# Moving work between VectorE, GpSimd and ScalarE in a state-space mixer, with taps over two blocks, a ring of six products and a new order

## The chip, the cores and the metric

The kernel runs on one core of one Trainium2 chip. The metric is the device time of one execution in microseconds; the kernel before is given by three runs and one profiled execution. The engines are named TensorE (PE in the rows; PEld is its weight load), VectorE (DVE), ScalarE (ACT), GpSimd (POOL) and SyncE (SP, which only issues DMAs here).

## The reference

The input is a batch of 8 sequences of 256 tokens with 256 features. After a layer norm two branches read it, and their results are added to the input: a state-space mixer and an MLP of six blocks.

```python
zxbcdt = hidden_states @ W_in                  # z, x: 4096 channels each; B, C: 128; dt: 64 heads
xbc = _causal_conv1d(xbc, conv_w, conv_b)      # 4 taps over time, then silu
dt = jax.nn.softplus(dt + dt_bias)
dA_cs = jnp.cumsum(dt * A, axis=2)
L = jnp.exp(jnp.where(mask, dA_cs[i] - dA_cs[j], -jnp.inf))       # causal decay
Y = jnp.einsum('bcign,bcjgn,bcijgh,bcjghp->bcighp', Cm, Bm, L, dtx) # plus the states of earlier chunks
y = (Y + D * x) * _silu(z)
yn = y * jax.lax.rsqrt(jnp.mean(y * y) + EPS) * norm_w
x = x + yn @ W_out + _L0_ffn_ref(xn)           # 6 x (W1, gelu, W2, residual, layer norm)
```

The kernel does not run the chunked scan: a sequence is only 256 tokens long, so it takes the whole causal 256 x 256 decay matrix of each sequence and head at once.

## The kernel before

The program has three parts: `prepare` (layer norm, B, C, dt and their running sums), `mix` (the mixer) and `mlp`. The change touches `mix` alone.

**Tiles, blocks, products.** `mix` goes over 32 tiles `c` of 128 inner channels, which are two heads (HPT = 2) of 64. Within a tile the 2048 tokens are four blocks `b` of 512 (NB = 4), each two sequences `s` of 256 (SPB = 2). What this document calls a product is one pair (b, s): for both heads, the causal decays times C.B of one sequence, eight per tile. The causal matrix of 256 x 256 is held as 128 partitions (source tokens) by LW = 384 columns: first source half against all 256 targets, then second source half against the last 128. Two heads make 768 columns. The columns 128 to 256 of each head lie wholly below the diagonal.

**The way of a tile.** TensorE projects x (`project_x`) and z (`project_z`), each block six matmuls 512 wide into one of two PSUM banks `pa`; ScalarE turns the x bank into the convolution's first term (`conv0`, L847), VectorE adds the three other taps (`tap`, helper `conv_tap`, L517) straight from the bank, ScalarE applies silu (`silu_x`, L856), and for z silu out of the bank (`silu_z`, L865). A bank is free again after the third tap, or after the silu of z. TensorE transposes x to token rows (`tokens`, L750), ScalarE copies them (`copy_tokens`, L892).

Beside it run the decays: VectorE writes the exponents of a product (`exponents`, L989: for each head one instruction 256 and one 128 wide) into the ring `dec`, clipped by the constant `floor`, which lies in PSUM; ScalarE takes the exponential in place (`decays`, L874, 768 wide); GpSimd multiplies by the masked C.B in `gmat` (`times_g`, L681, 768 wide). TensorE then multiplies with the token rows (`outputs`, L769), VectorE adds D x (`add_dx`, L1004) and gates with silu(z) (`gate`, L1017), ScalarE squares (`square`, L883) and rounds (`high`, L919), GpSimd sums the squares (`add_square`, L690) and forms the low part (`low`, L670). Every second tile TensorE begins the rows of W_out for the pair of tiles before (`output_rows`, L787 to L789, twelve matmuls 256 wide in a piece), and VectorE adds them to `acc` (`add_rows`, L1030). Weights are split in a high and a low part by `w_hi`, `o_hi` (ScalarE) and `w_lo`, `o_lo` (GpSimd, L654 and L662); `scale_o` (L901) applies the norm's weight.

**What sets the order.** Each engine has a function `step(c)` in which the order of one tile's steps is written out by hand, with tiles mixed: a step of tile c stands beside steps of c - 1 and c + 1. The engines run their lists independently and wait for semaphore counts. `wait_past` leaves a wait out where the count is zero or less. `dec` holds four products (two blocks), so `exponents` waits for the product of two blocks back. SyncE loads the rows of running sums `srow` in two halves of a tile, 512 KB for each head, once VectorE has written the exponents of that half (`arg_done`); its queue is in order with the other loads of `body`. The weights of the MLP's first layer go to `w1raw`, loaded at the mixer's start.

## Time and profile before

| | us |
|---|---|
| median of 3 runs | 1522.66 (1520.12 to 1525.63) |
| profiled execution, its own time | 1524.01 |
| its span | 1522.2 |
| busy over the span: TensorE / VectorE / ScalarE / GpSimd | 1448.4 / 1255.7 / 1087.8 / 1119.7 |
| mixer's first exponents / its last instruction on VectorE | 75.0 / 947.0 |

The profiled span is shown as 40 slices of 38 us, each digit the busy tenths of a slice:

```profile
DVE  6899999999999999999999993567666776776752
ACT  5679888888988888898888883656555555655542
POOL 4279999999999999999999997645263451634650
PEclk9899999999999999999999997999999999999999
```

The first two slices are `prepare`, the next twenty-two the mixer, the rest the MLP. TensorE's busy time says little here, since the ends of its matmuls are modelled: its demand is read from the starts. An operation on VectorE, ScalarE and GpSimd is shown with its own length, and the next one may start some 0.05 to 0.1 us before it ends, so a row's cost in a full queue is the distance between two starts.

### The profile page before, as it was taken

To read this page: it belongs to the slowest core of one execution; us is meant where nothing else is said; L and a number is where in the kernel's file an instruction comes from. 1 tells how busy PE (TensorE), PEld (TensorE's weight loads), DVE (VectorE), ACT (ScalarE), POOL (GpSimd) and SP (SyncE) were. 2 spreads that over 40 slices of the span, in tenths; PEclk is the share of its full clock that TensorE was granted. 3 is DMA by queue.
4 is the path that set the end of the run, shared out by engine and by line. 5 is a ranking of instruction groups with operands and counts; after the bars stand their busy time and mean duration, and the time that the engine had idled before them with its cause. 6 is when DMAs were issued, how large, how long until landed. Compare 5 with 4: busy or idle time off the path is not lost. (4 is left out here: it accounts for less than half of the span.)

```text
span 1522.2 us, 27373 instructions
## 1 busy us (share of the span) xinstructions
PE 1448.4 (95%) x9432; PEld 1188.4 (78%) x9432; DVE 1255.7 (82%) x2534; ACT 1087.8 (71%) x1764; POOL 1119.7 (74%) x763
## 2 busy tenths in 40 slices
PE   6789999999999999999999997999999999999998
PEld 5556777777777777777777776899998989989988
DVE  6899999999999999999999993567666776776752
ACT  5679888888988888898888883656555555655542
POOL 4279999999999999999999997645263451634650
PEclk9899999999999999999999997999999999999999
DMA  4233323232332323232232210300101001020011
GB/s 142 72 130 105 97 79 105 83 105 91 105 98 74 102 90 105 91 105 98 70 100 96 98 56 26 128 1 29 39 2 66 0 28 38 0 79 0 1 56 42
DMA packets 50159, 107.62 MB, mean 71 GB/s; under 512 B 13248, under 2 KB 25792, under 8 KB 48448
## 3 DMA queue, kind: packets, MB, share of 16 engines
q1 hardware_dynamic: 50048, 106.21, 21.3%
q8 instruction: 61, 1.00, 0.3%
q14 instruction: 50, 0.41, 0.1%
HBM read 101.47 MB, written 4.72 MB: 70 GB/s over the span
## 5 line engine op out<-in xcount | busy, mean ns | idle before, releaser
L681 POOL TENSOR_TENSOR mix_dec<-mix_dec,gmat 128x768 f32<-128x768 f32 x256 | 471.1, 1862 | 17.1 <-ACT mix_dec L874 17.1
L1411 DVE TENSOR_TENSOR mlp_hlo<-mlp_h,mlp_hhi 128x512 fp32r<-128x512 f32 x192 | 209.6, 1093 | 181.9 <-ACT mlp_hhi L1343 181.5
L989 DVE SCALAR_TENSOR_TENSOR mix_dec<-srow,tokpar,mix_floor 128x256 f32<-128x256 f32 (+1 forms) x1024 | 348.9, 408 | 11.9 <-PE mix_py L769 11.9
L1338 ACT ACTIVATE mlp_h<-mlp_p,mlp_b1c 128x512 f32<-128x512 f32 x192 | 132.1, 688 | 203.4 <-PE mlp_p L501 197.5
L517 DVE SCALAR_TENSOR_TENSOR xt<-mix_pa,conv,xt 128x510 f32<-128x510 f32 x372 | 262.3, 740 | 12.3 <-ACT xt L847 9.6
L501 PE MATMUL mix_pa<-xhi,whi 128*128 128x512 f32 x496 | 212.8, 429 | 20.5 <-DVE xt L517 19.6
L769 PE MATMUL mix_py<-mix_dec,mix_xtok 128*64 128x256 f32 (+1 forms) x2048 | 215.0, 339 | 15.9 <-ACT mix_xtok L892 8.6
L1304 PE MATMUL mlp_p<-mlp_w2hi,mlp_hhi 128*128 128x256 f32 x768 | 218.6, 285 | 3.2 <-DVE acc L1470 3.2
L1306 PE MATMUL mlp_p<-mlp_w2hi,mlp_hlo 128*128 128x256 f32 x768 | 216.5, 282 | 0.0
L769 PEld LDWEIGHTS mix_py<-mix_dec,mix_xtok 128*64 128x64 f32 x2048 | 128.4, 137 | 112.2 <-issue 57.8
L1305 PE MATMUL mlp_p<-mlp_w2lo,mlp_hhi 128*128 128x256 f32 x768 | 216.0, 281 | 0.0
L874 ACT ACTIVATE mix_dec<-mix_dec 128x768 f32<-128x768 f32 x256 | 212.9, 844 | 3.8 <-DVE mix_dec L989 2.8
L501 PE MATMUL mix_pa<-xlo,whi 128*128 128x512 f32 x496 | 196.7, 397 | 0.0
L501 PE MATMUL mix_pa<-xhi,wlo 128*128 128x512 f32 x496 | 196.6, 396 | 0.0
L690 POOL TENSOR_TENSOR mix_sqacc<-mix_sqacc,mix_sq 128x512 f32<-128x512 f32 x128 | 166.6, 1302 | 4.5 <-ACT mix_sq L883 4.5
L670 POOL TENSOR_TENSOR mix_glo<-mix_yg,mix_ghi 128x512 fp32r<-128x512 f32 x128 | 167.4, 1308 | 1.9 <-ACT mix_ghi L919 1.9
L501 PE MATMUL mlp_p<-xhi,mlp_w1hi 128*128 128x512 f32 x384 | 153.5, 400 | 2.0 <-POOL mlp_w1lo L1199 2.0
L1304 PEld LDWEIGHTS mlp_p<-mlp_w2hi,mlp_hhi 128*128 128x128 f32 x768 | 144.6, 188 | 13.4 <-DVE mlp_hlo L1411 3.6
L501 PE MATMUL mlp_p<-xlo,mlp_w1hi 128*128 128x512 f32 x384 | 153.3, 399 | 0.0
L501 PE MATMUL mlp_p<-xhi,mlp_w1lo 128*128 128x512 f32 x384 | 153.2, 399 | 0.0
L787 PE MATMUL mix_po<-mix_ohi,mix_ghi 128*128 128x256 f32 x512 | 148.6, 290 | 3.5 <-POOL mix_glo L670 2.1
L1305 PEld LDWEIGHTS mlp_p<-mlp_w2lo,mlp_hhi 128*128 128x128 f32 x768 | 144.6, 188 | 6.1
(130 smaller groups left out, 3207.8 us busy)
## 6 DMA issues: line engine op xcount, KB each, us to landing
srow<-cs_rows SPq DMA_DIRECT2D x128, 512.0 KB, 4.6
wraw<-w_xz SPq DMA_DIRECT2D x32, 256.0 KB, 5.6
w1raw<-w SPq DMA_DIRECT2D x6, 1028.0 KB, 4.8
mlp_w2raw<-w SPq DMA_DIRECT2D x6, 1024.0 KB, 6.7
mix_oraw<-w_out SPq DMA_DIRECT2D x16, 257.0 KB, 5.5
prep_hid<-hidden SPq DMA_DIRECT2D x4, 512.0 KB, 6.6
xn_rows<-prep_hid SPq DMA_DIRECT2D x4, 512.0 KB, 2.9
mlp_res<-xn_rows SPq DMA_DIRECT2D x1, 2048.0 KB, 10.2
```

What stands on the lines that cost most here:

```text
L501: last = pe.matmul(dst, w[:, k, :], x[:, k, cols], start=(i == 0), stop=(i == len(passes) - 1))
L517: return dve.scalar_tensor_tensor(d[:, :, k:SEQ], s[:, :, 0:SEQ - k], weight, d[:, :, k:SEQ], ALU.mult, ALU.add)
L670: pool.tensor_tensor(glo[:, t.par, cols(b)], yg[:, b, :], ghi[:, t.par, cols(b)].bitcast(F32), ALU.subtract).then_inc(glo_done, 1)
L681: pool.tensor_tensor(d, d, g, ALU.mult).then_inc(g_done, 1)
L690: pool.tensor_tensor(sqacc[:, cols(b)], sqacc[:, cols(b)], sq[:, b % 2, :], ALU.add).then_inc(sq_added, 1)
L769: last = pe.matmul(py[b % 2][hp, i], xtok[:, b % 2, 2 * s + j, hp], dec[:, b % 2, s, h, m], start=(j == 0), stop=(j == 1))
L874: act.activation(d, d, ACT.Exp, scale=-1.0).then_inc(dec_done, 1)
L989: last = dve.scalar_tensor_tensor(dec[:, b % 2, s, h, k], srow[:, half, h, i], tokpar[:, tile, HPT * c + h:HPT * c + h + 1], floor[:, 0:1] ...
L1304: pe.matmul(dst, hhi[:, j, k], w2hi[:, j, :], start=(j == 0), stop=False)
L1305: pe.matmul(dst, hhi[:, j, k], w2lo[:, j, :], start=False, stop=False)
L1306: last = pe.matmul(dst, hlo[:, j, k], w2hi[:, j, :], start=False, stop=(j == KH - 1))
L1411: dve.tensor_tensor(hlo[:, j, :], h[:, j % 4, :], hhi[:, j, :].bitcast(F32), ALU.subtract).then_inc(hlo_done, 1)
```

## The change

All of it is in `mix`, on four engines and the DMA queue.

```diff
+        DVE_G = [3]
+        POOL_G = [u for u in range(SPB * NB) if u not in DVE_G]
...
+        spare = w1raw[:, 0:SPB * HPT * LW].rearrange("p (s h i) -> p s h i", s=SPB, h=HPT)
...
+        def ring(c, b):
+            n = (NB * c + b) % 3
+            return dec[:, n] if n < 2 else spare
...
             load(0, d_par, dcol[:, 0], d_in[0])
-            sp.dma_start(w1raw[:], w1[0]).then_inc(w1_in, 16)
...
-                            sp.wait_ge(arg_done, SPB * (NB * c + NB // 2 * (half + 1)))
+                            sp.wait_ge(dec_done, SPB * (NB * c + NB // 2 * (half + 1)))
...
+            last = max(n for n in range(NB * NCT) if n % 3 == 2)
+            sp.wait_ge(y_done, SPB * (last + 1))
+            sp.dma_start(w1raw[:], w1[0]).then_inc(w1_in, 16)
...
-                pe.wait_ge(g_done, SPB * n + s + 1)
+                if u in DVE_G:
+                    pe.wait_ge(dve_g_done, len(DVE_G) * t.c + DVE_G.index(u) + 1)
+                else:
+                    pe.wait_ge(pool_g_done, len(POOL_G) * t.c + POOL_G.index(u) + 1)
...
             def decays(c, b, s):
...
-                d = dec[:, b % 2, s].rearrange("p h i -> p (h i)")
-                act.activation(d, d, ACT.Exp, scale=-1.0).then_inc(dec_done, 1)
+                if s == 0:
+                    d = ring(c, b)[:, s].rearrange("p h i -> p (h i)")
+                    act.activation(d, d, ACT.Exp, scale=-1.0).then_inc(dec_done, 1)
+                    return
+                half, i1 = b // 2, b % 2 * BLK + s * SEQ + P
+                tile = b * TPB + 2 * s
...
+                for h in range(HPT):
...
+                    act.activation(ring(c, b)[:, s, h, P:SEQ], srow[:, half, h, i1:i1 + P], ACT.Exp,
+                                   bias=tokpar[:, tile, HPT * c + h:HPT * c + h + 1], scale=-1.0)
+                d = ring(c, b)[:, s].rearrange("p h (k i) -> p h k i", i=P)[:, :, 0:3:2, :]
+                act.activation(d, d, ACT.Exp, scale=-1.0).then_inc(dec_done, 1)
...
-            def tap(c, b, k):
+            def taps(c, i, k):
...
-                conv_tap(dve, xt[:, t.par, cols(b)], pa[b % 2][:],
-                         conv[:, t.par, TAPS - 1 - k:TAPS - k], k).then_inc(done, 1)
+                conv_tap(dve, xt[:, t.par, 2 * i * BLK:2 * (i + 1) * BLK], pab[:],
+                         conv[:, t.par, TAPS - 1 - k:TAPS - k], k).then_inc(done, 2)
...
-                wait_past(dve, y_done, m - 2 * SPB + 1)
+                wait_past(dve, y_done, m - 3 * SPB + 1)
...
+                    first = SEQ if s == 0 else P
...
+            def times_g(c, b, s):
...
+                dve.wait_ge(dec_done, SPB * (NB * t.c + b) + s + 1)
+                d = ring(c, b)[:, s]
+                g = gmat[:, b * SPB + s, :].unsqueeze(1).broadcast_to([P, HPT, LW])
+                dve.tensor_tensor(d, d, g, ALU.mult).then_inc(dve_g_done, 1)
```

In words: product (1, 1) of each tile, number 3 of eight, is multiplied by the masked C.B on VectorE and no longer on GpSimd, both operands in SBUF; TensorE waits for one of two counts, one for each of these engines. In the second product of each block (s = 1) VectorE no longer writes the exponents of the columns 128 to 256; ScalarE computes their exponential from the row of running sums with the token's number as bias. The two banks become one tensor `pab`, and each tap is one instruction over both. The ring holds three blocks, the third in the memory of `w1raw`, whose load comes at the end of the mixer. The load of the next rows waits for the exponentials of the half instead of its exponents. And each engine's `step(c)` is written in a new order. Three places of it follow; `w1raw` in the rows of after is the third block of the ring.

VectorE, the middle of a tile, before: the taps of blocks 2 and 3, one bank a row, between D x, gate and one product's exponents.

```order
L517 SCALAR_TENSOR_TENSOR xt<-mix_pa0,conv,xt 128x2x255 [waits conv0_done]
L1004 SCALAR_TENSOR_TENSOR mix_py0<-xt,mix_dcol,mix_py0 128x512 [waits mix_y_done,mix_d_in0]
L517 SCALAR_TENSOR_TENSOR xt<-mix_pa0,conv,xt 128x2x254 [waits tap1_done]
L1017 TENSOR_TENSOR mix_yg<-mix_py0,zt 128x512 [waits mix_sq_done,mix_glo_done,z_done,mix_yd_done]
L989 SCALAR_TENSOR_TENSOR mix_dec<-srow,tokpar,mix_floor 128x256 [waits mix_y_done]
L989 SCALAR_TENSOR_TENSOR mix_dec<-srow,tokpar,mix_floor 128x128
L989 SCALAR_TENSOR_TENSOR mix_dec<-srow,tokpar,mix_floor 128x256
L989 SCALAR_TENSOR_TENSOR mix_dec<-srow,tokpar,mix_floor 128x128
L517 SCALAR_TENSOR_TENSOR xt<-mix_pa1,conv,xt 128x2x255 [waits conv0_done]
L517 SCALAR_TENSOR_TENSOR xt<-mix_pa0,conv,xt 128x2x253 [waits tap2_done]
L517 SCALAR_TENSOR_TENSOR xt<-mix_pa1,conv,xt 128x2x254 [waits tap1_done]
L517 SCALAR_TENSOR_TENSOR xt<-mix_pa1,conv,xt 128x2x253 [waits tap2_done]
```

The same engine after, from the end of block 3's first exponents on: the product by C.B (L1025) stands between the two products of exponents, and the taps take both banks at once.

```order
L1012 SCALAR_TENSOR_TENSOR w1raw<-srow,tokpar,mix_floor 128x128
L1025 TENSOR_TENSOR mix_dec<-mix_dec,gmat 128x768 [waits mix_dec_done]
L1012 SCALAR_TENSOR_TENSOR w1raw<-srow,tokpar,mix_floor 128x128 [waits mix_y_done]
L1012 SCALAR_TENSOR_TENSOR w1raw<-srow,tokpar,mix_floor 128x128 x3
L1036 SCALAR_TENSOR_TENSOR mix_py0<-xt,mix_dcol,mix_py0 128x512 [waits mix_y_done,mix_d_in0]
L517 SCALAR_TENSOR_TENSOR xt<-mix_pab,conv,xt 128x4x255 [waits conv0_done]
L1049 TENSOR_TENSOR mix_yg<-mix_py0,zt 128x512 [waits mix_sq_done,mix_glo_done,z_done,mix_yd_done]
L517 SCALAR_TENSOR_TENSOR xt<-mix_pab,conv,xt 128x4x254 [waits tap1_done]
L1036 SCALAR_TENSOR_TENSOR mix_py1<-xt,mix_dcol,mix_py1 128x512 [waits mix_y_done]
L517 SCALAR_TENSOR_TENSOR xt<-mix_pab,conv,xt 128x4x253 [waits tap2_done]
```

What moved: the exponents of block 3 stand ahead of the tile's second taps, and the operation L1025, which waits for ScalarE, is new among them. The six rows of taps are three.

ScalarE, the end of block 3, before:

```order
L919 CAST mix_ghi<-mix_yg 128x512 [waits mix_o_done,mix_gated]
L892 COPY mix_xtok<-mix_pt 128x512 [waits mix_y_done,mix_xtok_done]
L874 ACTIVATE mix_dec<-mix_dec 128x768 [waits mix_arg_done]
L847 ACTIVATE xt<-mix_pa1,conv 128x512 [waits mix_yd_done,px_done]
L919 CAST mix_ghi<-mix_yg 128x512 [waits mix_o_done,mix_gated]
L874 ACTIVATE mix_dec<-mix_dec 128x768 [waits mix_arg_done]
```

and after:

```order
L904 ACTIVATE mix_sq<-mix_yg 128x512 [waits mix_sq_added,mix_gated]
L940 CAST mix_ghi<-mix_yg 128x512 [waits mix_o_done,mix_gated]
L856 ACTIVATE xt<-mix_pab,conv 128x512 [waits mix_yd_done,px_done] x2
L884 ACTIVATE mix_dec<-mix_dec 128x768 [waits mix_arg_done]
L892 ACTIVATE mix_dec<-srow,tokpar 128x128 [waits mix_arg_done]
L892 ACTIVATE mix_dec<-srow,tokpar 128x128
L895 ACTIVATE mix_dec<-mix_dec 128x2x2x128
```

What moved: the biases of blocks 2 and 3 (`conv0`) stand together ahead of the exponentials of block 3, and the second exponential is three instructions.

GpSimd, around the first six products of a tile, before:

```order
L681 TENSOR_TENSOR mix_dec<-mix_dec,gmat 128x768 [waits mix_dec_done]
L670 TENSOR_TENSOR mix_glo<-mix_yg,mix_ghi 128x512 [waits mix_ghi_done]
L681 TENSOR_TENSOR mix_dec<-mix_dec,gmat 128x768 [waits mix_dec_done] x2
L690 TENSOR_TENSOR mix_sqacc<-mix_sqacc,mix_sq 128x512 [waits mix_sq_added,mix_sq_done]
L681 TENSOR_TENSOR mix_dec<-mix_dec,gmat 128x768 [waits mix_dec_done] x3
L654 TENSOR_TENSOR wlo<-wraw,whi 128x512 [waits mix_w_hi_done]
L690 TENSOR_TENSOR mix_sqacc<-mix_sqacc,mix_sq 128x512 [waits mix_sq_added,mix_sq_done]
```

and after:

```order
L687 TENSOR_TENSOR mix_dec<-mix_dec,gmat 128x768 [waits mix_dec_done] x2
L687 TENSOR_TENSOR w1raw<-w1raw,gmat 128x768 [waits mix_dec_done]
L687 TENSOR_TENSOR mix_dec<-mix_dec,gmat 128x768 [waits mix_dec_done]
L676 TENSOR_TENSOR mix_glo<-mix_yg,mix_ghi 128x512 [waits mix_ghi_done]
L687 TENSOR_TENSOR mix_dec<-mix_dec,gmat 128x768 [waits mix_dec_done] x2
L696 TENSOR_TENSOR mix_sqacc<-mix_sqacc,mix_sq 128x512 [waits mix_sq_added,mix_sq_done]
L660 TENSOR_TENSOR wlo<-wraw,whi 128x512 [waits mix_w_hi_done]
L676 TENSOR_TENSOR mix_glo<-mix_yg,mix_ghi 128x512 [waits mix_ghi_done]
```

What moved: the sum of squares that stood between the products is gone from there, a product is missing (the one on VectorE), and the low part of the block before stands ahead of product (2, 1), waiting for ScalarE's rounded part.

## Rows read from the trace of the kernel before

**Rows 1.** Stretch, length; busy us of PE, PEld, DVE, ACT, POOL; clock, DMA, GB/s.

```profile
400.00:600.00 200.00, 195.28 (x1336) 150.11 (x1334) 195.59 (x421) 173.35 (x275) 196.87 (x132) 1.00 0.28 90
```

**Rows 2.** Timeline of ScalarE: start us, length us, engine, line, operation, count.

```profile
424.80 0.78 ACT L847 ACTIVATE xt<-mix_pa,conv 128x512 f32<-128x512 f32 x1 [0.30 <-PE mix_pa L501]
...
451.50 0.78 ACT L847 ACTIVATE xt<-mix_pa,conv 128x512 f32<-128x512 f32 x1 [0.30 <-PE mix_pa L501]
```

**Rows 3.** One line: ns min/median/max, first and last start; then VectorE's timeline.

```profile
L681 POOL TENSOR_TENSOR mix_dec<-mix_dec,gmat x256: 1808/1862/1925, 77.4 to 924.0; 128x768 f32<-128x768 f32 x128
...
947.04 0.17 DVE L1069 TENSOR_SCALAR meansq<-mix_pt 128x16 f32<-128x16 f32 x1 [2.78 <-PE mix_pt L822]
```

**Rows 4.** Waits, 400 to 608 us: who for whom, us in total, times, longest.

```profile
POOL mix_dec L681 <- ACT mix_dec L874: 3.1, 4, 0.8
...
DVE xt L517 <- ACT xt L847: 1.7, 7, 0.2
...
PE mix_pa L501 <- DVE xt L517: 5.2, 8, 0.7
```

**Rows 5.** Timeline of TensorE.

```profile
406.52 0.66 PE L750 MATMUL mix_pt<-ident,xt 128*128 128x128 f32 x4
...
406.94 0.36 PE L787 MATMUL mix_po<-mix_ohi,mix_ghi 128*128 128x256 f32 x1
...
408.45 0.39 PE L501 MATMUL mix_pa<-xhi,whi 128*128 128x512 f32 x1
...
409.94 1.63 PE L769 MATMUL mix_py<-mix_dec,mix_xtok 128*64 128x256 f32 x16
...
411.50 0.66 PE L750 MATMUL mix_pt<-ident,xt 128*128 128x128 f32 x4
...
415.12 0.43 PE L501 MATMUL mix_pa<-xhi,whi 128*128 128x512 f32 x1
...
416.56 0.39 PE L501 MATMUL mix_pa<-xhi,whi 128*128 128x512 f32 x1
```

**Rows 6.** Timeline of GpSimd.

```profile
434.91 1.88 POOL L681 TENSOR_TENSOR mix_dec<-mix_dec,gmat 128x768 f32<-128x768 f32 x1
436.72 1.30 POOL L662 TENSOR_TENSOR mix_olo<-mix_oraw,mix_ohi 128x512 fp32r<-128x512 f32 x1
```

**Rows 7.** Timeline of VectorE and of GpSimd in the MLP.

```profile
984.79 0.69 DVE L1411 TENSOR_TENSOR mlp_hlo<-mlp_h,mlp_hhi 128x512 fp32r<-128x512 f32 x1 [2.14 <-ACT mlp_hhi L1343]
...
1063.36 2.40 POOL L1218 TENSOR_TENSOR mlp_res<-mlp_u,mlp_grow 128x1024 f32<-128x1024 f32 x1 [1.50 <-DVE mlp_u L1441]
...
1065.84 2.72 POOL L1220 TENSOR_TENSOR mlp_res<-mlp_res,mlp_grow 128x1024 f32<-128x1024 f32 x1
...
1063.83 2.48 DVE L1411 TENSOR_TENSOR mlp_hlo<-mlp_h,mlp_hhi 128x512 fp32r<-128x512 f32 x1 [0.55 <-ACT mlp_hhi L1343]
```

**Rows 8.** Groups of instructions, 400 to 608 us (busy, mean ns), and VectorE's timeline.

```profile
L989 DVE SCALAR_TENSOR_TENSOR mix_dec<-srow,tokpar,mix_floor 128x256 f32<-128x256 f32 x126 | 59.8, 475 | 2.1 <-PE mix_py L769 2.1
...
L989 DVE SCALAR_TENSOR_TENSOR mix_dec<-srow,tokpar,mix_floor 128x128 f32<-128x128 f32 x126 | 43.0, 341 | 0.0
...
400.17 2.69 DVE L517 SCALAR_TENSOR_TENSOR xt<-mix_pa,conv,xt 128x508 f32<-128x508 f32 x4
...
402.78 0.68 DVE L1017 TENSOR_TENSOR mix_yg<-mix_py,zt 128x512 f32<-128x512 f32 x1
```

**Rows 9.** Timeline of ScalarE.

```profile
406.85 0.84 ACT L874 ACTIVATE mix_dec<-mix_dec 128x768 f32<-128x768 f32 x1
...
407.58 0.63 ACT L883 ACTIVATE mix_sq<-mix_yg 128x512 f32<-128x512 f32 x1
...
408.61 0.92 ACT L901 ACTIVATE mix_oraw<-mix_oraw 128x256 f32<-128x256 f32 x2
...
409.42 0.61 ACT L919 CAST mix_ghi<-mix_yg 128x512 fp32r<-128x512 f32 x1
```

**Rows 10.** Loads (part 6 of the page): count, KB each, us to landing.

```profile
w1raw<-w SPq DMA_DIRECT2D x6, 1028.0 KB, 4.8
```

More of the change, by code:

```diff
@@ L533, in mix @@
         wraw, whi, wlo, w_in, conv, conv_in, srow, srow_in, xt, zt, stages, w1raw, w1_in, meansq):
-    DVE_G = [(0, 0)]
-    POOL_G = [(b, s) for b in range(NB) for s in range(SPB) if (b, s) not in DVE_G]
     with ExitStack() as ctx:
@@ L562, in mix @@
         onesq = sb("onesq", [P, 2])
-        pa = [ps(f"pa{i}") for i in range(2)]
+        pab = ctx.enter_context(nc.psum_tensor("mix_pab", [P, 2 * BLK], F32))
+        pa = [pab[:, i * BLK:(i + 1) * BLK] for i in range(2)]
         pt = ps("pt")
@@ L769, in outputs @@
                         last = pe.matmul(py[b % 2][hp, i], xtok[:, b % 2, 2 * s + j, hp],
-                                         dec[:, b % 2, s, h, m], start=(j == 0), stop=(j == 1))
+                                         ring(c, b)[:, s, h, m], start=(j == 0), stop=(j == 1))
                 last.then_inc(y_done, 1)
@@ L792, in step @@
             def step(c):
+                project_x(c, 1)
+                output_rows(c - 1, 0)
+                tokens(c - 1, 1)
+                output_rows(c - 1, 1)
+                tokens(c - 1, 2)
+                outputs(c - 1, 0, 0)
+                outputs(c - 1, 0, 1)
+                project_x(c, 2)
+                project_x(c, 3)
+                output_rows(c - 1, 2)
+                outputs(c - 1, 1, 0)
+                outputs(c - 1, 1, 1)
+                tokens(c - 1, 3)
+                output_rows(c - 1, 3)
                 outputs(c - 1, 2, 0)
-                tokens(c - 1, 3)
                 outputs(c - 1, 2, 1)
+                tokens(c, 0)
                 project_z(c, 0)
@@ L931, in step @@
                 conv0(c + 1, 0)
-                high(c - 1, 1)
                 conv0(c + 1, 1)
@@ L983, in exponents @@
                     dve.wait_ge(srow_in[half], 16 * HPT * (t.c + 1))
-                wait_past(dve, y_done, m - 2 * SPB + 1)
+                wait_past(dve, y_done, m - 3 * SPB + 1)
                 for h in range(HPT):
-                    for j, i, k in ((0, slice(i0, i0 + SEQ), slice(0, SEQ)),
+                    first = SEQ if s == 0 else P
+                    for j, i, k in ((0, slice(i0, i0 + first), slice(0, first)),
                                     (1, slice(i0 + P, i0 + SEQ), slice(SEQ, LW))):
@@ L989, in exponents @@
                         last = dve.scalar_tensor_tensor(
-                            dec[:, b % 2, s, h, k], srow[:, half, h, i],
+                            ring(c, b)[:, s, h, k], srow[:, half, h, i],
                             tokpar[:, tile, HPT * c + h:HPT * c + h + 1],
@@ L993, in exponents @@
                 last.then_inc(arg_done, 1)
+            def times_g(c, b, s):
+                if not 0 <= c < NCT:
+                    return
+                t = tile_of(c)
+                dve.wait_ge(dec_done, SPB * (NB * t.c + b) + s + 1)
+                d = ring(c, b)[:, s]
+                g = gmat[:, b * SPB + s, :].unsqueeze(1).broadcast_to([P, HPT, LW])
+                dve.tensor_tensor(d, d, g, ALU.mult).then_inc(dve_g_done, 1)
             def add_dx(c, b):
```

148 lines of the change are left out of this document (66 added, 82 removed).

## Prediction

> **What bounds the kernel now.** I read the page's table of slices first: VectorE, ScalarE and GpSimd are dense up to the 24th slice and thin behind it, so the program is a mixer of some 870 us and an MLP of some 575 us, and the change touches the mixer alone. The view by stretches shows it in the steady middle [rows 1]: of 200 us GpSimd is busy 196.87, VectorE 195.59, ScalarE 173.35, and TensorE 195.28 by a modelled end. Then I took one tile's length: the same ScalarE row comes again after 451.50 - 424.80 = 26.70 us [rows 2]. The products run from 77.4 to 924.0 us and the mixer to 947 [rows 3]; 846.6 us is 31 tiles of 26.70 and the 19 us of the last. So each 0.1 us of a tile is worth 3.1 us of the kernel.
>
> Per tile the busy shares become GpSimd 0.984 x 26.70 = 26.28 us, VectorE 26.11, ScalarE 23.14. The waits in 208 us [rows 4] are few: GpSimd 3.1 us for the exponentials, 0.4 per tile; that and its 26.28 us make up the 26.70. GpSimd is therefore the bound, VectorE is 0.2 us behind it, and TensorE waits 5.2 us (0.65 per tile) for the taps to free a bank. TensorE's own demand is read off from where its groups start [rows 5]: the first projection of a run takes 1.49 us (408.45 to 409.94), one that follows another 1.44 (415.12 to 416.56); twelve output-row matmuls 1.51 (406.94 to 408.45); four transposes 0.42 (406.52 to 406.94); two C.B products 1.56 (409.94 to 411.50). The granted clock is 1.00 in that stretch [rows 1], the upper level, so these are its prices.
>
> **The change, part by part**, each as microseconds per tile.
>
> *One product of eight to VectorE.* GpSimd loses one of its eight. Its price there is the distance of two starts, 436.72 - 434.91 = 1.81 [rows 6]. GpSimd: 26.28 - 1.81 = 24.47. No row of before has VectorE do this product. The nearest is VectorE's subtraction with both inputs in SBUF in the MLP, 512 wide: 0.69 us [rows 7]. The exponents give the slope: 475 - 341 = 134 ns for 128 elements [rows 8], so 768 wide is 0.69 + 0.27 = 0.96, and 0.88 to the next start, since neighbours overlap by 0.08 (four taps are busy for 2.69 us, and the next operation starts after 2.61 [rows 8]). But [rows 7] show a second thing. The same subtraction, started at 1063.83 while GpSimd's 2.40 us operation of 1063.36 ran, took 2.48 and ended 0.55 us behind GpSimd's end; GpSimd's next, started at 1065.84, took 2.72. They exclude each other for the whole instruction. In the mixer of before this never shows, since each VectorE operation there has one input in PSUM. So the product costs VectorE 0.88 and a wait between 0 and one GpSimd product, 1.8. Walking the new order in starts from the third tap of blocks 0 and 1 at 0: the product is due at 3.1; GpSimd is by then 0.3 us from the end of its fourth product, and waits behind it for the high part of the gated block. I take 0.3, keep 0 and 1.8, and charge GpSimd nothing, as VectorE's 0.88 falls into a gap of about 1.1 us in which GpSimd waits for ScalarE; without that gap it costs GpSimd 0.9, for which its 1.2 us below TensorE's demand has room.
>
> The Trainium skill, "SBUF — State Buffer", section "Who interferes with whom", speaks against handing work between these two: VectorE with two SBUF inputs and a GpSimd instruction that reads SBUF hold the pair of ports for a whole instruction, and the second fully blocks. By that rule alone the move gives GpSimd 1.81 - 0.88 and not 1.81. The rows of the MLP agree with the rule.
>
> *Half of the exponentials below the diagonal to ScalarE.* VectorE's second product of each block computes 128 instead of 256 exponents for both heads: 4 blocks x 2 x 0.134 = 1.07 saved. ScalarE splits that block's exponential: two 128-wide ones with bias and scale from the row, and a 512-wide one for the rest in place of 768. Spacings of starts [rows 9]: 768 wide 0.73 (406.85 to 407.58); 512 wide 0.51 (two rows from 407.58 to 408.61, halved); with a pointer operand and 256 wide 0.405 (0.81 for two from 408.61 to 409.42). By ScalarE's slope of 0.22/256 per element, 128 wide is 0.405 - 0.11 = 0.29. So 2 x 0.29 + 0.51 - 0.73 = 0.36 more, four times: 1.44. Its bounds are 1.1 (short ones at 0.25) and 2.4 (at 0.41, the 256-wide price). ScalarE: 23.14 + 1.44 = 24.6.
>
> The Trainium skill, "ScalarE: Activation LUTs", section "What ACT_TABLE_LOAD costs", gives a 128-wide ACTIVATE with pointer bias 280 + 0.833 x 128 = 387 ns, of which neighbours hide 93. That is 0.294 each and would leave the sum as it is; no run yet shows the 128-wide form.
>
> *Taps over two blocks.* Twelve taps of 0.65 (2.61 / 4) become six. A doubled one adds 510 elements at 1.047 ns: 0.65 + 0.53 = 1.19. VectorE: 7.83 - 7.12 = 0.71 saved. What it costs is in the banks: both are given back only with the third tap.
>
> *Sum for VectorE:* 26.11 - 1.07 - 0.71 + 0.88 + 0.3 = 25.5, with 25.2 and 27.0 as ends.
>
> *Ring of six.* The exponents wait for a product six back, not four. The wait it lifts is the 2.1 us for TensorE's products at the end of the first row of [rows 8], 0.27 per tile, already in the gaps between busy and 26.70. The third block of the ring lies in the buffer of the MLP's first weights, whose 1 MB load moves from the mixer's start to the product two blocks before its end. Behind that are two blocks of products, their gates and the last rows, over 10 us, while this load lands in 4.8 us [rows 10], so I cost it at nothing; were it bare it would be 5 us, once. The row loads now wait for the exponential on ScalarE instead of the exponents on VectorE, a few us later: by the walk the first half is issued at 26 us and wanted at 37, and it is no larger than the load of [rows 10].
>
> *New order.* On TensorE the work is the same, in other groups: 3 runs of projections (3 x 1.49 + 5 x 1.44 = 11.67), output rows 4 x 1.51 = 6.04, products 4 x 1.56 = 6.24, transposes 4 x 0.42 = 1.68: 25.63 us. Of four engines this is now the largest, so it is the floor: TensorE 25.63, VectorE 25.5, ScalarE 24.6, GpSimd 24.5. Walked through with these prices, the loop that returns to itself is: third tap done, projections x 2 and 3, taps of blocks 2 and 3, four z projections, two products, projections x 0 and 1, bias on ScalarE, three taps. The work put between fills TensorE's waits to within 0.1 to 0.3 us at three places (x 2, z 0, and the tap behind x 1). Before, the kernel ran 0.4 above its largest sum. I take 0.15 above, 25.8, and keep 25.63 and 26.1.
>
> *Ends.* At the start six instead of four products of exponents precede the first taps, 1.8 us later (by [rows 8] a full one is 2 x (0.395 + 0.261) = 1.31 and a lessened one 1.04, so 7.05 for 5.24); at the end GpSimd has three operations of 1.25 between its last product and TensorE's last rows, four before. Net 0.5 us more.
>
> **Sum.** 31 x (26.70 - 25.8) = 27.9, less 0.5: 27.4 us. The profiled execution took 1524.0 us, its span 1522.2; it would become 1496.6. It stands 1.3 above the median of the three runs shown, so against the median the forecast is 1495 us, 1.8% faster.
>
> **Rivals.** (a) *The shared banks bind.* ScalarE gets no rest between the bias of block 1 and that of block 3: by the walk the latter is ready 0.5 us before the tap wants it. If the short exponentials cost 0.41, three of these blocks lie there and add 3 x 0.24 = 0.7; the doubled tap cannot start on the first bank alone, as a single one could. The tile becomes 26.2 to 26.6, say 26.4: 1514 us. For it: VectorE waits for this bias in the trace of before too, 1.7 us in 208 [rows 4]. Against: by the sum ScalarE still rests 1.2 us in a tile of 25.8, and the tap's 0.5 us have to be used up first.
>
> (b) *VectorE becomes the bound through the exclusion, and the kernel is slower.* The place is the product between two blocks of exponents; behind it on the same queue stand the exponents of block 3 and the tap for which TensorE waits. If the phase is such that it always meets a fresh GpSimd product, VectorE needs 27.0, and with the old 0.2 of gaps 27.2: 31 x 0.5 = 15.5 us slower, 1538. It decides from a wait of 1.3 us on. Against it: such a wait makes VectorE late, while GpSimd is 1.2 us under the floor and drifts ahead into its gap, where the port is free.
>
> (c) *It does not do what it says*: GpSimd's relief is real but VectorE stays as full as it was, at 26.5 with its waits: within 0.3%, 1520.
>
> (d) *Better*: the new order leaves TensorE no wait and a tile takes 25.5: 1486.
>
> **Chances.** Forecast (25.6 to 26.1 us per tile, 1486 to 1503) 0.60; (a) 0.16; (b) 0.09; (c) 0.07; (d) 0.08. A measurement of this kernel tells about 0.3% from no change. Faster is the forecast, (a) and (d): 0.84; same is (c), 0.07; slower (b), 0.09. The range reaches from (d) to the far side of (a), 1484 to 1517, and leaves out (b) and (c), 0.16.
>
> **What will show it.** Right: a tile of 25.8 between two equal rows in the middle; GpSimd's busy share at 0.95 or below with its waits on ScalarE, TensorE with almost none; the doubled tap at 1.27 us a piece; the short exponential near 0.38; VectorE's product between 0.96 and 1.3 on average. A product above 2 us with VectorE at 99% means (b); TensorE waiting over 0.5 us per tile for taps behind a late bias means (a). The MLP should keep its length to a microsecond. I would be wrong altogether if the row loads came too late at the exponents of a new tile, or if GpSimd's products grew beside the VectorE one.

## The result, and the profile after

The kernel after takes 1488.86 us, median of four runs (1488.68 to 1494.12); the kernel before, four runs beside it, 1521.66 (1520.12 to 1525.63). The ratio is 0.979, its 95% interval 0.9775 to 0.9799: 2.1% faster, where 1.8% was forecast (1495 us, range 1484 to 1517). The profiled execution of after took 1488.68 us, with a span of 1486.9.

First the view by stretches, over the same 200 us as [rows 1], and the waits of 400 to 608 us (who for whom: us in total, times, longest), to be held beside [rows 4]:

```profile
400.00:600.00 200.00, 198.11 (x1364) 159.20 (x1363) 197.08 (x400) 189.67 (x348) 192.21 (x130) 1.00 0.30 100
...
ACT zt L874 <- PE mix_pab L501: 7.8, 8, 1.1
POOL mix_glo L676 <- ACT mix_ghi L940: 7.3, 8, 1.1
...
PEld mix_pab L501 <- DVE xt L517: 2.4, 8, 0.3
DVE xt L517 <- ACT xt L856: 2.1, 8, 0.3
PE mix_pt L755 <- ACT mix_xtok L913: 1.7, 5, 0.4
```

GpSimd fell from 196.87 to 192.21 busy, and now waits for ScalarE's rounded part, about 0.9 us per tile. ScalarE rose from 173.35 to 189.67; it still waits for TensorE's z projections (7.8 us, before 10.3), while its wait for TensorE's token transposes, 14.7 us before, is gone from the list. What is left on TensorE's side are 1.7 us for token copies and short waits of its weight loads. Second, one tile's length. Each exponential table load of ScalarE stands once in a tile; the timeline of ScalarE (start, length) gives three tiles:

```profile
409.43 1.28 ACT L884 ACT_TABLE_LOAD   x1
...
434.90 1.28 ACT L884 ACT_TABLE_LOAD   x1
...
460.75 1.28 ACT L884 ACT_TABLE_LOAD   x1
...
486.22 1.28 ACT L884 ACT_TABLE_LOAD   x1
```

The distances are 25.47, 25.85 and 25.47: the tile alternates, where before it was 26.70 each time [rows 2]. Two tiles are 51.32, the mean about 25.67. Third, the mixer's ends on VectorE, its first exponents and its last instruction (before: 75.0 and 947.04, [rows 3]):

```profile
73.19 3.98 DVE L1012 SCALAR_TENSOR_TENSOR mix_dec<-srow,tokpar,mix_floor 128x256 f32<-128x256 f32 x13
...
914.06 0.17 DVE L1096 TENSOR_SCALAR meansq<-mix_pt 128x16 f32<-128x16 f32 x1 [2.77 <-PE mix_pt L831]
```

So of the 35.3 us between the two profiled spans (1522.2 and 1486.9) the mixer gave 872.0 - 840.9 = 31.1, the part ahead of it 1.8 and the MLP 2.4 (575.2 and 572.8), though no instruction of those two was changed.

Fourth, the new operations: VectorE with the doubled taps and the product (L1025), then GpSimd at the same time, then ScalarE's split exponential.

```profile
441.94 1.26 DVE L517 SCALAR_TENSOR_TENSOR xt<-mix_pab,conv,xt 128x1012 f32<-128x1012 f32 x1
...
443.71 1.38 DVE L1012 SCALAR_TENSOR_TENSOR w1raw<-srow,tokpar,mix_floor 128x256 f32<-128x256 f32 x4
445.01 1.55 DVE L1025 TENSOR_TENSOR mix_dec<-mix_dec,gmat 128x768 f32<-128x768 f32 x1
446.48 1.11 DVE L1012 SCALAR_TENSOR_TENSOR w1raw<-srow,tokpar,mix_floor 128x128 f32<-128x128 f32 x4
...
442.08 3.66 POOL L687 TENSOR_TENSOR mix_dec<-mix_dec,gmat 128x768 f32<-128x768 f32 x2
446.83 1.29 POOL L676 TENSOR_TENSOR mix_glo<-mix_yg,mix_ghi 128x512 fp32r<-128x512 f32 x1 [1.09 <-ACT mix_ghi L940]
...
413.10 0.68 ACT L892 ACTIVATE mix_dec<-srow,tokpar 128x128 f32<-128x128 f32 x2
413.68 0.62 ACT L895 ACTIVATE mix_dec<-mix_dec 128x512 f32<-128x512 f32 x1
```

The product begins 0.73 us before GpSimd's pair ends at 445.74, is itself 1.55 long and ends 0.82 behind that end, in the gap of 1.09 that the prediction had named.

### The profile page after: what moved, and what is told of

Same layout as the page of the kernel before. It is cut to its first block and busy times, and to the rows that moved or that the text cites. A ratio compares the mean times of both kernels' runs of the same rounds, so it can differ in the third digit from the quotient of the medians.

```text
span 1486.9 us, 27692 instructions
## 1 busy us (share of the span) xinstructions
PE 1424.6 (96%) x9432; PEld 1198.3 (81%) x9432; DVE 1237.1 (83%) x2380; ACT 1126.7 (76%) x2020; POOL 1064.4 (72%) x731
## 5 line engine op out<-in xcount | busy, mean ns | idle before, releaser
L1438 DVE TENSOR_TENSOR mlp_hlo<-mlp_h,mlp_hhi 128x512 fp32r<-128x512 f32 x192 | 218.1, 1138 | 175.8 <-ACT mlp_hhi L1370 175.6
L687 POOL TENSOR_TENSOR mix_dec<-mix_dec,gmat 128x768 f32<-128x768 f32 x151 | 278.1, 1856 | 10.4 <-ACT mix_dec L884 6.8
L517 DVE SCALAR_TENSOR_TENSOR xt<-mix_pab,conv,xt 128x1020 f32<-128x1020 f32 x186 | 236.2, 1270 | 12.7 <-ACT xt L856 9.2
L1012 DVE SCALAR_TENSOR_TENSOR mix_dec<-srow,tokpar,mix_floor 128x128 f32<-128x128 f32 (+1 forms) x688 | 214.2, 373 | 1.9 <-PE mix_py L778 1.9
L501 PE MATMUL mix_pab<-xhi,whi 128*128 128x512 f32 x496 | 206.0, 415 | 2.0 <-DVE xt L517 0.2
L501 PE MATMUL mix_pab<-xlo,whi 128*128 128x512 f32 x496 | 196.5, 396 | 0.0
L501 PE MATMUL mix_pab<-xhi,wlo 128*128 128x512 f32 x496 | 196.5, 396 | 0.0
L676 POOL TENSOR_TENSOR mix_glo<-mix_yg,mix_ghi 128x512 fp32r<-128x512 f32 x128 | 164.7, 1299 | 31.4 <-ACT mix_ghi L940 30.4
L797 PE MATMUL mix_po<-mix_olo,mix_ghi 128*128 128x256 f32 x512 | 146.0, 285 | 0.0
L798 PE MATMUL mix_po<-mix_ohi,mix_glo 128*128 128x256 f32 x512 | 145.7, 285 | 0.0
L1333 PEld LDWEIGHTS mlp_p<-mlp_w2hi,mlp_hlo 128*128 128x128 f32 x768 | 144.5, 188 | 0.0
```

What stands on the lines that cost most here:

```text
L501: last = pe.matmul(dst, w[:, k, :], x[:, k, cols], start=(i == 0), stop=(i == len(passes) - 1))
L517: return dve.scalar_tensor_tensor(d[:, :, k:SEQ], s[:, :, 0:SEQ - k], weight, d[:, :, k:SEQ], ALU.mult, ALU.add)
L676: pool.tensor_tensor(glo[:, t.par, cols(b)], yg[:, b, :], ghi[:, t.par, cols(b)].bitcast(F32), ALU.subtract).then_inc(glo_done, 1)
L687: pool.tensor_tensor(d, d, g, ALU.mult).then_inc(pool_g_done, 1)
L797: pe.matmul(dst, ghi[:, e, r], olo[:, e, :], start=False, stop=False)
L1012: last = dve.scalar_tensor_tensor(ring(c, b)[:, s, h, k], srow[:, half, h, i], tokpar[:, tile, HPT * c + h:HPT * c + h + 1], floor[:, 0:1] ...
```

## The experiments

All times are medians of the runs made, with the ratio to the kernel before and its interval; the kernel before gave 1521.65 to 1522.21 beside them. "Tile" is the distance of exponential table loads in the middle of the mixer.

**Theory:** each of the three vector engines has a total per tile, the longest set 26.70 before, and the moves bring all of them under TensorE's. **Rivals:** the order and the ring alone do it; the exclusion of VectorE and GpSimd through SBUF eats the gain.

### Single moves undone in the kernel after

*pool8*: the product back on GpSimd.

```diff
-        DVE_G = [3]
+        DVE_G = []
...
                 times_g(c, 1, 0)
+                times_g(c, 1, 1)
                 times_g(c, 2, 0)
...
                 exponents(c - 1, 3, 0)
-                times_g(c - 1, 1, 1)
                 exponents(c - 1, 3, 1)
```

> The changed kernel with one part undone: product (1,1) goes back to GpSimd, behind (1,0); VectorE has none. Theory (sums): GpSimd is again the largest at 24.5 + 1.8 = 26.3 us per tile and waits once for ScalarE's rounded part (0.9 us per tile after the change), so a tile takes 26.3 to 27.2 and the kernel 1489 + 31 x (0.6 to 1.5) = 1508 to 1536 us, GpSimd at 97% or more. Rival (the order and the ring brought the gain, not this part): 1489 to 1494, with TensorE still without waits.

Measured: 1513.41 us, 0.9945 (0.9928 to 0.9962). Tiles alternate between 25.8 and 26.9, mean 26.34. The stretch 400 to 600, then the same for *fullexp*, which gives the 128 columns below the diagonal back to VectorE (1507.79 us, 0.9906, 0.9889 to 0.9922; tile 26.26):

```profile
400.00:600.00 200.00, 196.23 (x1346) 155.18 (x1346) 184.44 (x386) 184.22 (x337) 199.76 (x134) 1.00 0.31 98
```

```profile
400.00:600.00 200.00, 193.89 (x1343) 156.10 (x1343) 199.27 (x391) 175.42 (x279) 193.41 (x127) 1.00 0.30 98
```

```diff
-                if s == 0:
+                if True:
...
-                    first = SEQ if s == 0 else P
+                    first = SEQ
```

> The changed kernel with one part undone: VectorE writes all exponents, ScalarE takes each exponential in one 768-wide piece. Theory (sums): VectorE was at 25.3 us busy of 25.67 per tile and gets 1.07 back, so it becomes the bound at 26.4 and the kernel takes 1489 + 31 x 0.75 = 1512 us (1505 to 1520), while ScalarE falls below 90%. Rival: ScalarE is what limits the changed kernel (it is busy 95% there), and relieving it of 1.4 us pays for VectorE's 1.07: 1485 to 1495.

In the first GpSimd has 199.76 of 200 us, in the second VectorE 199.27: undoing one move fills exactly the engine that gets the work back. Both moves are needed, and each is worth about 0.6 us of a tile, since the other engine is just behind.

*onetaps*: twelve single taps again, for six doubled ones.

```diff
             def taps(c, i, k):
+                tap(c, 2 * i, k)
+                tap(c, 2 * i + 1, k)
...
-                dve.wait_ge(before, NB * c + 2 * i + 2)
-                conv_tap(dve, xt[:, t.par, 2 * i * BLK:2 * (i + 1) * BLK], pab[:],
-                         conv[:, t.par, TAPS - 1 - k:TAPS - k], k).then_inc(done, 2)
+                dve.wait_ge(before, NB * c + b + 1)
+                conv_tap(dve, xt[:, t.par, cols(b)], pa[b % 2],
+                         conv[:, t.par, TAPS - 1 - k:TAPS - k], k).then_inc(done, 1)
```

> The changed kernel with one part undone: each tap is two instructions again, one per bank, in the same place. Theory (sums): VectorE gets 0.7 us per tile back, 26.0 instead of 25.3 busy, so the kernel takes 1489 + 31 x (0.4 to 0.7) = 1501 to 1511 us. Rival (joining the banks costs time, because a bank is given back late): single taps free the first bank 0.6 us sooner and start on the first bias alone, which pays for their length: 1480 to 1492.

Measured: 1490.35 us (1488.89 to 1496.95), 0.9783 (0.9766 to 0.9799), the same time as after; tile 25.67. VectorE's row and its groups of 400 to 608 us (busy, mean ns):

```profile
400.00:600.00 200.00, 198.78 (x1369) 159.27 (x1368) 200.00 (x446) 190.29 (x347) 193.75 (x130) 1.00 0.30 98
...
L1029 DVE TENSOR_TENSOR mix_dec<-mix_dec,gmat 128x768 f32<-128x768 f32 x5 | 6.1, 1217 | 0.0
...
L517 DVE SCALAR_TENSOR_TENSOR xt<-mix_pab,conv,xt 128x510 f32<-128x510 f32 (+2 forms) x100 | 69.6, 753 | 0.0
```

The taps cost 69.6 us instead of 62.2, and VectorE is full to the last tenth, but not longer than TensorE's tile. The price is smaller than the row suggests, since neighbours overlap. From start to next start, over sixteen tiles between 330 and 760 us, the taps cost 7.85 us a tile against 7.31 in after: 0.54 more, not 0.71. VectorE paid for it with the 0.26 us per tile that it waited in after, with 0.09 of a gap behind the gates, and with a product that waits less for GpSimd (1.09 against 1.25 from start to start). My expectation of 1501 to 1511 missed. The time is what its rival gave; whether the rival's reason, a start on the first bias alone, has a part in the lost wait, these rows do not tell. *dve_probe*, with joined taps, lost the same wait: one more 128-wide exponent operation on VectorE per tile, its result unused.

```diff
                 last.then_inc(arg_done, 1)
+                if (b, s) == (3, 1):
+                    last = dve.scalar_tensor_tensor(
+                        floor[:, P:2 * P], srow[:, half, 0, i],
+                        tokpar[:, tile, HPT * c + h:HPT * c + h + 1],
+                        floor[:, 0:1].broadcast_to([P, k.stop - k.start]), ALU.subtract, ALU.max)
```

> The changed kernel with one more 128-wide exponent instruction on VectorE in block 3 of each tile, written to unused PSUM, 0.26 us more work per tile. Theory (TensorE is the floor, VectorE 0.3 us below it): 1489 to 1492. Rival (VectorE is the floor, its waits being only the exclusion's): 1489 + 31 x 0.26 = 1497.

Measured: 1493.41 us (1489.36 to 1499.84), 0.98 (0.9785 to 0.9815), tiles 25.47 and 25.86 as in after. The median lies between the theory's 1489 to 1492 and the rival's 1497, and the four runs spread over 10 us, so the time decides nothing. The tile does: the extra operation costs 0.26 us from start to start, VectorE's wait of 0.26 per tile is gone, and the tile is as long as in after.

### The floor, and the longer of two tiles

*pe_probe*: block 3 is transposed twice, by my estimate 0.36 us more for TensorE.

```diff
-                for k in range(b * TPB, (b + 1) * TPB):
+                for k in [j for _ in range(1 + (b == 3)) for j in range(b * TPB, (b + 1) * TPB)]:
```

> The changed kernel with TensorE's four transposes of block 3 done twice, 0.36 us more work per tile and nothing else. Theory (TensorE's demand is the floor): a tile takes 0.3 to 0.36 longer, 1489 + 31 x 0.33 = 1498 to 1500 us. Rival (VectorE's or ScalarE's row of work is what a tile takes): TensorE has the room, 1489 to 1491.

Measured: 1498.51 us, 0.9843; the tile is 25.90 each time. Against 25.47 and 25.87 that is 0.43 in the shorter tile and 0.03 in the longer. In pe_probe the two sets of transposes take 0.84 us (452.71 to 453.55) where one takes 0.41 in after, so 0.43 is the probe's whole price: the shorter tile is TensorE's own. The longer has 0.4 us of something else. TensorE's timeline of after shows what. First the shorter tile, then the longer:

```profile
425.68 1.52 PE L778 MATMUL mix_py<-mix_dec,mix_xtok 128*64 128x256 f32 x16
427.13 0.66 PE L755 MATMUL mix_pt<-ident,xt 128*128 128x128 f32 x4
...
451.15 1.52 PE L778 MATMUL mix_py<-mix_dec,mix_xtok 128*64 128x256 f32 x16
453.01 0.63 PE L755 MATMUL mix_pt<-ident,xt 128*128 128x128 f32 x4 [0.35 <-ACT mix_xtok L913]
```

Transposes come 1.45 us behind the products, or 1.86 when TensorE waits for ScalarE's copy of the tokens before. Only every second tile scales W_out (L922, two operations, 0.90 us busy), and they stood ahead of this copy. *scale_late* puts them behind it:

```diff
                 decays(c, 2, 1)
-                scale_o(c + 1)
                 square(c - 1, 2)
                 copy_tokens(c, 2)
...
                 high(c - 1, 3)
+                scale_o(c + 1)
                 silu_z(c + 1, 0)
```

> The changed kernel with one step moved on ScalarE: the scaling of the output weights (two 256-wide rows, every second tile) from behind the exponentials of block 2 to just ahead of the silu of z block 0, where ScalarE waits about 1 us for TensorE. The changed kernel's tiles take 25.47 and 25.87 us in turn. Theory (in the longer tile ScalarE's unbroken row of work is late by the scaling, so TensorE waits 0.35 us for the copied tokens): all tiles take 25.47, so 16 x 0.4 = 6 us less than the changed kernel, 1482 to 1484 us. Rival (the longer tile comes from GpSimd's low part of the weights or from TensorE's own demand of 25.6): no change, 1488 to 1490.

Measured: 1486.03 us (1484.86 to 1492.10, five runs), 0.9768 (0.9749 to 0.9786), some 3 us below after, though the intervals overlap. I had expected 1482 to 1484 with every tile at 25.47. The tile is 25.48 and 25.60, so 0.27 of the 0.40 went, and the wait for the copy is gone from the list of 400 to 608 us. The 0.13 that stays lies in TensorE's row behind the same products: there the four transposes take 0.51 us to the next start and not 0.41, and the projections behind them 5.81 and not 5.78; no run says why.

```profile
435.02 1.28 ACT L884 ACT_TABLE_LOAD   x1
...
460.62 1.28 ACT L884 ACT_TABLE_LOAD   x1
...
486.09 1.28 ACT L884 ACT_TABLE_LOAD   x1
```

### The ring

*ring4*: the new order with the old ring of two blocks.

```diff
-            n = (NB * c + b) % 3
-            return dec[:, n] if n < 2 else spare
+            return dec[:, b % 2]
...
-                wait_past(dve, y_done, m - 3 * SPB + 1)
+                wait_past(dve, y_done, m - 2 * SPB + 1)
```

> The changed kernel with one part undone: the ring holds four products, the exponents wait for the product of two blocks back. Theory: the new order needs the third block. By the starts of the changed kernel the exponents of block 1 are due some 2.5 us before the product of block 3 of the tile before, for which they would wait, and this stands ahead of the next taps: 2 to 4 us per tile, 1550 to 1610 us. Rival (the ring only lifted the 0.27 us per tile of waits that were there before): 1489 to 1500.

Measured: 1965.04 us, 1.291 (1.289 to 1.293); the tile is 40.95. The waits of 400 to 608 us:

```profile
DVE mix_dec L1011 <- PE mix_py L777: 78.4, 20, 7.3
POOL mix_dec L686 <- ACT mix_dec L883: 50.6, 13, 8.8
PEld mix_pab L501 <- DVE xt L517: 43.0, 10, 7.8
```

VectorE's exponents wait for TensorE's product four back, 78.4 us in 208 or 15.4 per tile, and the tile grew by 15.3; behind them on the queue stand the taps for which TensorE's projections wait. The new order lets the exponents run further ahead than a ring of four can hold. I had priced the wait and not the loop that it closes, so the expected 1550 to 1610 was far off. The prediction had costed the ring at nothing but 0.27 us of waits; in truth the new order cannot do without it. What a ring of six gives in the old order no run shows.

### Order without moves, moves without order

*order_only* is after with the product on GpSimd, full exponents and single taps (the three edits above together). *b_dveprod* and *b_both* start from the kernel before. The first moves the product from GpSimd's step to VectorE's; the second does that and adds the lessened exponents (last line), with the split exponential of the change in `decays` and the row loads behind the exponentials. Both keep the single taps:

```diff
                 times_g(c, 1, 0)
-                times_g(c, 1, 1)
...
                 exponents(c, 2, 1)
+                times_g(c, 1, 1)
                 add_rows(c, 1)
...
+                first = SEQ if s == 0 else P
```

> The kernel after with all four moved loads undone at once: product (1,1) on GpSimd, full exponents on VectorE, single taps. The ring of six and the new order alone remain. Theory (each engine of vectors has its own total, and the longest sets the tile): GpSimd is again at the total it had with its product back, 26.3 us a tile, VectorE has 26.26 less the product's 1.1 plus 0.3 for the taps, about 25.5. So the tile is 26.3 to 26.45 and the time 1508 to 1519, as with the product alone back; VectorE waits, and ScalarE's busy time in 400 to 600 falls to about 170. Rival (order and ring bring nothing without the moves): tile 26.70, 1520 to 1524.

> The kernel before with one edit: product (1,1) on VectorE, behind the exponents of (2,1); old order, ring of four, full exponents, single taps. Theory (VectorE has no room: it was busy 195.6 of 200 us before): VectorE's total of 26.1 takes another 1.1, so the tile is 26.9 to 27.4 and the time 1530 to 1545, slower than before; GpSimd has waits. Rival (GpSimd alone bound the kernel before): tile 26.0 to 26.4, time 1500 to 1513. Third possibility, from what the ring of four did in the new order: the wait for a product two blocks back closes a loop, and the tile grows past 28, over 1560.

> The kernel before with product (1,1) on VectorE and the exponential of the 128 columns below the diagonal on ScalarE for s = 1, in the old order with the ring of four and single taps: the moves without ring and order. Theory (the moves make the room, the order turns it into time): VectorE has 26.1 plus 1.1 less 8 x 0.134 = 26.1 us of work, so at best 26.2 to 26.7 a tile, with waits for C.B products of two blocks back: 1508 to 1525. Rival 1 (the moves alone do it): tile 25.7, 1488 to 1495. Rival 2 (the ring of four closes a loop as in the new order): tile over 28, over 1560.

| | order and ring | product on | below the diagonal | tile | time | ratio (interval) |
|---|---|---|---|---|---|---|
| before | old | GpSimd | VectorE | 26.70 | 1521.7 | 1 |
| order_only | new | GpSimd | VectorE | 26.34 | 1511.23 | 0.9929 (0.9913 to 0.9946) |
| b_dveprod | old | VectorE | VectorE | 30.2 | 1627.45 | 1.0698 (1.068 to 1.0716) |
| b_both | old | VectorE | ScalarE | 27.1 | 1531.60 | 1.0063 (1.0047 to 1.008) |
| after | new | VectorE | ScalarE | 25.67 | 1488.86 | 0.9787 (0.9775 to 0.9799) |

Tiles are means: those of order_only alternate between 25.8 and 26.9, those of b_dveprod are 30.4 with a 28.9 now and then. The new order and ring alone bring 10 us, the two moves alone lose 10, and after, with joined taps besides, gains 33. Joined taps were worth nothing in the new order (onetaps); in the old one they were not tried. Order_only ran with GpSimd at 199.75 of 200, as the theory said: the order had only the old engine's waits to take away. B_both has room on the three vector engines (the stretch 400 to 600 and two waits):

```profile
400.00:600.00 200.00, 196.81 (x1313) 148.45 (x1311) 190.42 (x418) 180.37 (x331) 185.66 (x122) 1.00 0.29 93
...
POOL mix_dec L682 <- ACT mix_dec L879: 12.6, 12, 1.4
...
DVE xt L517 <- ACT xt L851: 8.4, 16, 0.9
```

VectorE is busy 190.4 and GpSimd 185.7 of 200: in the old order the room turns into waits. My 1508 to 1525 was too low by 7.

B_dveprod, which I expected at 1530 to 1545, is where the exclusion shows: two engines whose operations overlap in time, and one is held up until the other's instruction ends. VectorE and GpSimd in one tile of it:

```profile
441.29 2.51 DVE L1005 TENSOR_TENSOR mix_dec<-mix_dec,gmat 128x768 f32<-128x768 f32 x1
...
441.16 4.33 POOL L682 TENSOR_TENSOR mix_dec<-mix_dec,gmat 128x768 f32<-128x768 f32 x2 [1.06 <-ACT mix_dec L878]
```

GpSimd started 0.13 us earlier, and VectorE's product took 2.51 (2.50 at the median of the mixer), while GpSimd's pair took 4.33 and not the 3.66 of after. In b_both the same two meet the other way round:

```profile
436.28 0.95 DVE L1017 TENSOR_TENSOR mix_dec<-mix_dec,gmat 128x768 f32<-128x768 f32 x1
...
436.41 2.52 POOL L682 TENSOR_TENSOR mix_dec<-mix_dec,gmat 128x768 f32<-128x768 f32 x1 [0.90 <-ACT mix_dec L879]
```

Now VectorE was first, took 0.95, and GpSimd's 1.85 became 2.52.

### The exclusion by itself

Two kernels keep the product on VectorE and change its second operand to a zero in PSUM, so that the instruction and its waits stay and its contribution to the output is left out: *port* in the kernel after, *b_port* in b_dveprod.

```diff
+            dve.memset(floor[:, 1:2], 0.0).then_inc(floor_set, 1)
...
-                g = gmat[:, b * SPB + s, :].unsqueeze(1).broadcast_to([P, HPT, LW])
+                g = floor[:, 1:2].unsqueeze(1).broadcast_to([P, HPT, LW])
```

> The changed kernel with VectorE's product of each tile taken with a constant zero in PSUM instead of the masked C.B in SBUF, so that only one input lies in SBUF; this product's contribution is thereby left out. Theory (two SBUF inputs exclude GpSimd): the product takes 0.96 us each time instead of 1.1 to 1.9, and since VectorE and GpSimd are both below the floor, the kernel keeps its time, 1487 to 1490 us. Rival (the exclusion costs time on the path): 0.3 to 0.6 us per tile, 1470 to 1480.

> The kernel before with product (1,1) on VectorE at the same place as in b_dveprod, but its second operand is a zero held in PSUM, where C.B lies in SBUF: its contribution to the output is left out, the instruction and its waits stay. In b_dveprod the product took 2.50 us in nearly every tile against 0.95 in the few free ones, and the tile was 30.4 us (exponential table loads 400.87 to 521.10, four tiles in 120.2). Theory (two engines that both read SBUF twice hold each other up, and in a full VectorE queue that lies on the path): the product takes 0.95, the tile 28.3 to 29.0 (30.05 less 1.5, and less again where waits behind it shrink) and the time 1565 to 1590. Rival (the length of the product is not what the tile consists of; a loop of waits at the ring of four is): the product takes 0.95 and the tile stays at 29.5 to 30.5, time 1600 to 1628. Lowest: tile 27.1 as in b_both, 1531, if the hold was all of it.

VectorE's product by groups, 400 to 608 us, first of *port*, then of *b_port*:

```profile
L1026 DVE TENSOR_TENSOR mix_dec<-mix_dec,mix_floor 128x768 f32<-128x768 f32 x5 | 4.7, 944 | 0.0
```

```profile
L1006 DVE TENSOR_TENSOR mix_dec<-mix_dec,mix_floor 128x768 f32<-128x768 f32 x8 | 7.6, 951 | 0.0
```

In both it takes 0.95 us every time, whatever GpSimd does. *port* runs in 1488.66 us, 0.9781, with the tiles of after, 25.46 and 25.87: in the new order the exclusion lengthens the product by 0.15 to 0.6 us and costs no time. *b_port* runs in 1540.65 us, 1.0125 (1.0108 to 1.0142), its tile 27.36 and not 30.2: in the old order the exclusion costs 2.8 us a tile and 87 us in all, nearly twice the 1.55 by which the product grew. I had expected 28.3 to 29.0. In b_port GpSimd's products are short too, 1853 ns on average for 1932. The rest of the 2.8 us stands on VectorE's own row: in b_dveprod its exponents wait for TensorE's product of two blocks back, the old ring's wait,

```profile
DVE mix_dec L993 <- PE mix_py L773: 9.9, 6, 1.7
```

or 1.4 us per tile, and in b_port this wait is not in the list at all. So the delay came back through the ring. Other things were longer as well: TensorE's waits for VectorE's row additions (PE, L791) were 13.7 us in 208 and not 3.2, and the granted clock of the stretch was 0.95 and not 1.00. How much of the 1.4 each of them makes, no run separates.

## Why the prediction was right, point by point

**The bound.** That GpSimd bound, with VectorE close behind, is borne out by pool8 and fullexp, where either engine alone brings back 26.3, and by order_only, where GpSimd is full at 26.34. That TensorE takes over is shown by pe_probe, whose 0.43 us come back whole in the shorter tile, and by TensorE's row itself: in the shorter tile its groups follow each other from start to start without a marked wait. VectorE and the others are close under it: in onetaps VectorE is full at the same 25.67.

**The tile, 25.8 forecast, 25.67 measured.** The two terms in it were both mis-sized, in opposite directions. The floor of 25.63 was too high: a measured tile of 25.47 lies under it. From 425.68 to 451.15 the four groups of products took 5.94 (forecast 6.24; the first, 425.68 to 427.13 above, 1.45 for 1.56), the projections 11.59 (11.67), the output rows 6.20 (6.04) and the transposes 1.74 (1.68). So the products were priced too high, and the rows a little too low. The margin of 0.15 was too low: it is nothing in one tile and 0.4 in the next, and the 0.4 is the token copy behind the scaling of W_out, a place that my walk, which had no scaling of every second tile in it, did not name; scale_late took 0.27 of it away, the rest is open. That the two errors partly cancel, -0.16 and +0.05 on average, is luck of a small size. The difference of 0.13 is 31 x 0.13 = 4.0 us, the main part of what the forecast fell short.

**GpSimd.** Forecast at 24.47: 192.21 / 200 x 25.67 = 24.67. Its busy share is 0.96, not 0.95 or below. The waits are on ScalarE, as forecast.

**VectorE.** Forecast at 25.5: 197.08 / 200 x 25.67 = 25.3. The doubled tap is 1.27 us as forecast. The product is 1.33 on average in 400 to 608 us, just beyond the 0.96 to 1.3 given; it is about 1.1 in some tiles and 1.5 in most others; the wait behind GpSimd came where the walk put it and is 0.15 to 0.6 in all but three tiles, where it is 0.9 to 1.1; forecast 0.3. But the 0.71 that the taps were to save is 0.54 against single taps in the same order, and brought no time (onetaps): I summed it as if it were needed, and the sum without it, 26.2, was too high, since part of VectorE's stretch is wait that it can lose.

**ScalarE.** Forecast at 24.6: 189.67 / 200 x 25.67 = 24.3. The short exponential is 0.396 long and 0.29 from start to start (0.68 busy for two, 0.58 to the next start), the value taken; the sum by the Trainium skill ("ScalarE: Activation LUTs", section "What ACT_TABLE_LOAD costs"), 0.387 and 0.294, is confirmed by these rows.

**Ends.** Forecast 0.5 us lost: 31 x 1.03 = 31.9 and the mixer gave 31.1, so 0.8. The MLP did not keep its length to a microsecond: 2.4 shorter, and the part ahead of the mixer 1.8 shorter. The granted clock in these parts differs between executions; from 40 to 75 us, before and then after:

```profile
40.00:75.00 35.00, 25.55 (x99) 20.00 (x100) 28.99 (x48) 21.55 (x33) 8.32 (x9) 0.80 0.27 75
```

```profile
40.00:75.00 35.00, 24.88 (x107) 19.62 (x108) 29.93 (x54) 21.56 (x33) 9.01 (x10) 0.90 0.24 77
```

The clock alone does not explain it: port had 0.80 there, as before, and its mixer began at 72.95. Over the fourteen profiled kernels the mixer's first exponents came between 72.95 and 75.02 and the MLP ran 572.8 to 578.3 us, with the same code in both parts, so I take these 4.2 us for scatter of the profiled execution and no gain. They, 4.0 for the tile and -0.3 for the ends make up the 7.9 between the 27.4 forecast and the 35.3 seen between the spans; between the medians 32.8 were seen.

**The load of w1raw.** It is issued at 883.4 us and lands in 4.8 us as before [rows 10]; the MLP's first matmul starts at 916.0, 1.95 us behind the mixer's last instruction, and it was 1.95 before. In 400 to 608 us no engine waits for a row load.

**Rivals.** (a) would have needed TensorE to wait 0.5 us a tile for taps; the waits for them are 0.3. (b) did not happen here, but its mechanism is real: in the old order b_dveprod has it, a product that meets a fresh GpSimd product in 30 of 31 tiles, 2.50 us long, and the exclusion's part there, 87 us, is dearer than the 15.5 us I gave it. In the timeline of after the product stands at the end of a run of GpSimd products, ahead of its gap; that this place is what kept (b) away is my reading, since no run moves the product within the new order. The Trainium skill ("SBUF — State Buffer", section "Who interferes with whom") has the rule that a VectorE instruction with two SBUF inputs contends with a GpSimd instruction that reads SBUF, and that issue order decides who blocks. [rows 7] and these runs agree with it, and in port and after its price on the path is nothing. (c), a tile that stays at 26.5, is excluded by the tile itself. (d) stood at 25.5 and 1486: after is between it and the forecast, and scale_late, at 25.53 and 1486.03, is (d).

**Slips in the sums.** By the prediction's own rule of 31 tiles and 0.5 us, tiles of 25.6 to 26.1 give 1489 to 1505 and not 1486 to 1503, the far side of (a), 26.6, gives 1520 and not the range's 1517, and (c) gives 1517 and not 1520. None of this changes how the result is read: the measured tile of 25.67 lies within 25.6 to 26.1.

## What to carry to other kernels

Where three engines are within 2% of each other, moving work pays only if every one of them ends under the next bound, and only in an order that can spend the room: here the moves without the order cost 10 us, the order and ring without the moves gave 10, both gave 33. Before moving an operation with two SBUF operands to VectorE, look at what GpSimd does at that moment; placed just ahead of a gap of GpSimd it cost no time here, beside a fresh GpSimd operation in a full VectorE queue it cost 87 us. A tile whose length alternates points at work done every second time: find what stands behind it in the queue.
